# Staging rotary rows once per batch, and merging two norms into the projections behind them

## The reference, cut to what matters

```python
def _layernorm(x, axis=-1, eps=1e-05):
    ...
    return (x - m) / jnp.sqrt(v + eps)
...
c_kv = x @ W_kv_down
k_rope = _rotary_apply(c_kv @ W_k_rope, cos, sin)
k = (c_kv @ W_k_up).reshape(Bb, Tt, NH, HD)
v = (c_kv @ W_v_up).reshape(Bb, Tt, NH, HD)
q = (x @ W_q).reshape(Bb, Tt, NH, HD)
q_rope = _rotary_apply(x @ W_q_rope, cos, sin)
scores = jnp.einsum('bqhd,bkhd->bhqk', q, k)
scores = scores + jnp.einsum('bqr,bkr->bqk', q_rope, k_rope)[:, None]
...
w = jax.nn.softmax(scores, axis=-1)
attn = jnp.einsum('bhqk,bkhd->bqhd', w, v).reshape(Bb, Tt, D_MODEL)
```

## Time and profile before

| | us |
|---|---|
| median of three runs (3166.22 to 3172.92) | 3166.6 |
| the profiled execution, its time | 3168.85 |
| its span, first to last instruction | 3167.1 |
| PE busy in the span | 2359.3 (74%) |
| DVE busy | 1765.2 (56%) |
| ACT busy | 1243.2 (39%) |
| GpSimd (POOL) busy | 403.3 (13%) |

### The profile page before, as it was taken

The page is one execution under the profiler, slowest core; times in us unless marked ns, Lnnn a source line. Parts: engine busy times, 40 slices in busy tenths (PEclk is TensorE's granted clock), DMA queues, the critical chain, the costliest instruction groups (busy, mean ns, idle before and its releaser), DMA issues. The chain is left out here.

```text
span 3167.1 us, 47671 instructions
## 1 busy us (share of the span) xinstructions
PE 2359.3 (74%) x13512; PEld 1228.0 (39%) x13512; DVE 1765.2 (56%) x5580; ACT 1243.2 (39%) x1983; POOL 403.3 (13%) x452
## 2 busy tenths in 40 slices
PE   3649999999956328866999999999677292877382
PEld 1114344343335126532443434444254271554262
DVE  3746666666344896356665656666365324576223
ACT  2405555455525644553444444444222141343141
POOL 0000000000003000000000000000043463033554
PEclk9859999999968659967999999999888596888686
DMA  3272444443030000243121121121220142000144
GB/s 114 87 143 43 85 85 85 86 81 64 11 103 1 4 0 11 72 124 111 47 58 50 44 55 42 51 61 37 69 73 21 52 141 82 3 4 15 40 138 129
DMA packets 177888, 199.67 MB, mean 63 GB/s; under 512 B 36384, under 2 KB 117920, under 8 KB 177568
## 3 DMA queue, kind: packets, MB, share of 16 engines
q1 hardware_dynamic: 160000, 173.72, 22.0%
q0 software_dynamic: 9216, 19.02, 1.8%
q10 hardware_dynamic: 8448, 4.20, 0.4%
HBM read 127.09 MB, written 69.76 MB: 62 GB/s over the span
## 5 line engine op out<-in xcount | busy, mean ns | idle before, releaser
L910 ACT ACTIVATE at_probs<-at_score 128x1024 f32<-128x1024 f32 (+7 forms) x1024 | 654.7, 651 | 870.3 <-PE at_score L835 535.4
L935 DVE CUSTOM_DVE_ANT_0 at_masked<-at_mx,g_maskw 128x512 bf16<-128x512 f32 (+3 forms) x1024 | 483.3, 486 | 182.9 <-PE at_mx L801 178.2
L801 PE MATMUL at_mx<-at_K,at_Q 96*128 96x512 bf16 (+7 forms) x1536 | 464.9, 343 | 117.7 <-DVE at_mpart L935 39.6
L833 PE MATMUL at_score<-at_Q,at_K 96*128 96x512 bf16 (+7 forms) x1536 | 503.2, 332 | 27.7 <-issue 15.8
L835 PE MATMUL at_score<-at_Q,at_K 98*128 98x512 bf16 (+7 forms) x1536 | 506.3, 330 | 0.0
L931 DVE TENSOR_REDUCE at_mpart<-at_mx 128x1 f32<-128x512 f32 x512 | 353.8, 691 | 260.6 <-PE at_mx L801 242.1
L855 PE MATMUL at_outp<-at_probs,at_vop 128*32 128x512 f32 (+6 forms) x3072 | 445.9, 498 | 0.0
L801 PEld LDWEIGHTS at_mx<-at_K,at_Q 120*128 120x128 bf16 (+1 forms) x1536 | 148.2, 98 | 437.7 <-DVE at_mpart L935 198.2
L833 PEld LDWEIGHTS at_score<-at_Q,at_K 120*128 120x128 bf16 (+1 forms) x1536 | 149.5, 97 | 337.6 <-issue 180.9
L838 PE MATMUL at_score<-g_maskkq,g_identb 128*128 128x128 bf16 x1024 | 225.5, 221 | 0.0
L1025 POOL MEMSET n_spread<- 16x128 f32 (+1 forms) x2 | 0.7, 355 | 1537.9 <-POOLq L636 1537.9
(11 more groups left out here) (478 smaller groups left out, 3427.2 us busy)
## 6 DMA issues: line engine op xcount, KB each, us to landing
at_Q<-q SPq DMA_DIRECT2D x192, 128.0 KB, 2.8
at_Q<-qr SPq DMA_DIRECT2D x72, 256.0 KB, 6.7
at_K<-kr SPq DMA_DIRECT2D x72, 256.0 KB, 8.3
q<-p_pieces SPq DMA_DIRECT2D x40, 384.0 KB, 3.3
at_K<-k SPq DMA_DIRECT2D x168, 64.0 KB, 2.2
buf<-g_zeros SPq DMA_DIRECT2D x32, 325.0 KB, 5.3
o<-at_osb SPq DMA_DIRECT2D x64, 128.0 KB
n_oc<-o SPq DMA_DIRECT2D x8, 1024.0 KB, 5.0
```

The source lines that it names most:

```text
L801: pe.matmul(bank[:, 0:hi - lo], Q0[0:R, g % 4, j, qt * P:(qt + 1) * P], K0[0:R, g % 4, j % KG, lo:hi], start=True, stop=True).then_inc(s_m ...
L833: pe.matmul(bank, K0[0:R0, g % 4, j % KG, kb * P:(kb + 1) * P], Q0[0:R0, g % 4, j, lo:hi], start=True, stop=False)
L910: act.activation(probs[:, kb % 2, j, kb * P:T], src, ACT.Exp, scale=cf.scale).then_inc(s_exp, 1)
L935: dve.tensor_tensor_reduce(masked[:, u % 2, 0:w], mx[:, u % 2, 0:w], k.maskw[:, CH - w:CH], 1.0, NEG, ALU.add, ALU.max, mpart[:, part, j, ...
```

## The change

In the attention of the first layer, the 144 broadcast loads go. SP loads the rotary pieces of a batch once, unrepeated, into a tile `stage` of 96 partitions (12 loads of 64 KB). From there they are copied to the four heads of each slot by on-chip copies of 96 partitions x 4096 elements: for the first batch two by DVE (slot 0 of `Q0`, `K0`), four by ACT (both slots of `Q1`, `K1`), six by GpSimd; for the later batches all twelve by GpSimd, each pair behind the value products that free the slot. SP loads the next batch's `stage` at the end of a batch's first group. The starting memsets go from GpSimd to DVE in both attentions, and SP waits for the first of them alone; DVE's first `values` moves behind the first group's maxima.

In both projections the norm's block goes; `project` makes a `Norm` and weaves it in. The norm of chunk ch + 1 and the statistics of chunk ch + 2 are made while chunk ch is projected, and the bank of the latent product serves for the turned tiles too. The LO pieces go from DVE to GpSimd, which SP's stores and the next chunk's `rest` now wait for. The loops over chunks are written out.

```diff
+        if cf.SR:
+            stage = c.sb("stage", [96, 2, 2, T], BF16)
+            s_stage = c.sem("shared_staged")
...
-        nsh = 6 if cf.SR else 3
+        nsh = 3
...
+        def stage_loads(sp, b):
+            for p in range(2):
+                for n, (pieces, slots) in enumerate(((qs, Q_SLOTS), (ks, K_SLOTS))):
+                    for s in range(3):
+                        sp.dma_start(stage[32 * s:32 * s + 32, p, n, :],
+                                     pieces[slots[p][s], :, ds(first_token(b), T)]).then_inc(s_stage, 16)
+
         def shared_loads(sp, p, b, Qt, Kt, sem):
+            if cf.SR:
+                return
             for s in range(3):
                 r0 = 32 * s
                 def src(pieces, piece, n):
                     return pieces[piece, :, ds(first_token(b), T)].unsqueeze(1).broadcast_to([32, n, T])
-                if cf.SR:
-                    sp.dma_start(Qt[r0:r0 + 32, :, :], src(qs, Q_SLOTS[p][s], G)).then_inc(sem, 16)
-                sp.dma_start(Kt[r0:r0 + 32, :, :], src(ks if cf.SR else kp, K_SLOTS[p][s], KG)).then_inc(sem, 16)
+                sp.dma_start(Kt[r0:r0 + 32, :, :], src(kp, K_SLOTS[p][s], KG)).then_inc(sem, 16)
...
-            sp.wait_ge(s_set, 3)
+            if cf.SR:
+                stage_loads(sp, 0)
+            sp.wait_ge(s_set, 1)
...
+                if cf.SR and g == 0 and ahead(b, g, GN):
+                    for i in range(4):
+                        wait(s_s0[i], 2 * (b + 1))
+                    for i in range(2):
+                        wait(s_s1[i], 2 * (b + 1))
+                    stage_loads(sp, ahead(b, g, GN)[0])
...
-            pool.memset(K1[SHIFT_ROW:SHIFT_ROW + 2, :, :, :], 1.0).then_inc(s_set, 1)
-            pool.wait_ge(s_set, 1)
-            pool.memset(vop[:], 0.0).then_inc(s_set, 1)
-            pool.wait_ge(s_set, 2)
-            pool.memset(vop[:, :, :, :, d:d + 1], 1.0).then_inc(s_set, 1)
+
+            def spread(b, g, p):
+                Qt, Kt, sem = ((Q0[:, g % 4], K0[:, g % 4], s_s0[g % 4]) if p == 0 else
+                               (Q1[:, g % 2], K1[:, g % 2], s_s1[g % 2]))
+                pool.wait_ge(s_pv, (b * GN + g) * 8 + (8 if p == 0 else 24))
+                pool.sem_inc(s_ppassed, 1)
+                for n, t in enumerate((Qt, Kt)):
+                    pool.tensor_copy(t[0:96, :, :], stage[:, p, n, :].unsqueeze(1).broadcast_to([96, G, T])).then_inc(sem, 1)
+
+            def step(b):
+                pool.wait_ge(s_stage, 16 * 12 * (b + 1))
+                pool.sem_inc(s_ppassed, 1)
+                spread(b, 0, 0)
+                spread(b, 1, 0)
+                spread(b, 0, 1)
+                spread(b, 2, 0)
+                spread(b, 1, 1)
+                spread(b, 3, 0)
+
+            if cf.SR:
+                pool.wait_ge(s_stage, 16 * 12)
+                spread(0, 1, 0)
+                spread(0, 2, 0)
+                spread(0, 3, 0)
+                with pool.Fori(1, NB) as b:
+                    step(b)
...
-                    pe.wait_ge(s_s0[g % 4], 16 * nsh * (b + 1))
+                    pe.wait_ge(s_s0[g % 4], (2 if cf.SR else 16 * nsh) * (b + 1))
...
+            if cf.SR:
+                act.wait_ge(s_stage, 16 * 12)
+                for i in range(2):
+                    for n, t in enumerate((Q1, K1)):
+                        act.activation(t[0:96, i], stage[:, 1, n, :].unsqueeze(1).broadcast_to([96, G, T]),
+                                       ACT.Copy).then_inc(s_s1[i], 1)
...
+            dve.memset(K1[SHIFT_ROW:SHIFT_ROW + 2, :, :, :], 1.0).then_inc(s_set, 1)
+            dve.memset(vop[:], 0.0).then_inc(s_set, 1)
+            dve.wait_ge(s_set, 2)
+            dve.memset(vop[:, :, :, :, d:d + 1], 1.0).then_inc(s_set, 1)
+            if cf.SR:
+                dve.wait_ge(s_stage, 16 * 12)
+                for n, t in enumerate((Q0, K0)):
+                    dve.tensor_copy(t[0:96, 0], stage[:, 0, n, :].unsqueeze(1).broadcast_to([96, G, T])).then_inc(s_s0[0], 1)
+            reduce_units(0, 0, NARROW, 0)
+            wide_maxima(0, 0)
             dve.wait_ge(s_set, 3)
             values(0, 0)
-            reduce_units(0, 0, NARROW, 0)
-            wide_maxima(0, 0)
             reduce_units(0, 1, NARROW, 0)
...
+        norm = Norm(nc, c, k, xs, linear_view(hT), lambda ch: latp[:])
...
-            dve_steps += [("rest", n)] + [("lo", n - 1)] * (n > 0)
+            dve_steps += [("rest", n)]
         act_steps += [("mid", NI - 1)]
-        dve_steps += [("lo", NI - 1), ("values", 0)]
+        dve_steps += [("values", 0)]
...
+        turn_at = next((n for n in order if items[n].from_latent), None)
...
-                        sp.wait_ge(s_dve, DVN * (ch + 1) + dve_at["lo", n])
+                        sp.wait_ge(s_lo, NI * ch + n + 1)
...
+            norm.turn(pe, 0)
+            for i in range(NC // 2):
...
-                    pe.wait_ge(s_act, ACN * ch + act_at["lat", 0])
+                    pe.wait_ge(norm.s_ev, ch + 1)
...
+                        if n == turn_at:
                             pe.wait_ge(s_act, ACN * (ch + 1) + act_at["lat", 0])
+                            if ch + 1 < NC:
+                                norm.turn(pe, ch + 1)
...
+                    if turn_at is None:
+                        pe.wait_ge(s_act, ACN * (ch + 1) + act_at["lat", 0])
+                        if ch + 1 < NC:
+                            norm.turn(pe, ch + 1)
...
+            norm.root(act, 0)
+            norm.normalise_rest(act, 0)
+            norm.evacuate(act, 0)
+            norm.root(act, 1)
...
                             act.activation(lat[0:latent_rows, g, :], latp[0:latent_rows, :], ACT.Copy).then_inc(s_act, 1)
+                            if ch + 1 < NC:
+                                norm.normalise_rest(act, ch + 1)
+                            if ch + 2 < NC:
+                                norm.root(act, ch + 2)
...
                             act.activation(pcs[n][:, g, HI, :], source(n, it, g), ACT.Copy).then_inc(s_act, 1)
+                            if n == 0 and ch + 1 < NC:
+                                norm.evacuate(act, ch + 1)
...
+            norm.statistics(dve, 0)
+            norm.normalise(dve, 0)
+            norm.statistics(dve, 1)
...
+                    if ch + 1 < NC:
+                        norm.normalise(dve, ch + 1)
+                    if ch + 2 < NC:
+                        norm.statistics(dve, ch + 2)
...
+                            if ch > 0:
+                                dve.wait_ge(s_lo, NI * (ch - 1) + n + 1)
...
-                        elif what == "lo":
-                            dve.wait_ge(s_act, ACN * (ch + 1) + act_at["mid", n])
-                            dve.wait_ge(s_dve, base + dve_at["rest", n])
-                            ins = dve.tensor_tensor(pcs[n][:, g, LO, :], rest[0:it.rows, n, :], pcs[n][:, g, MID, :], ALU.subtract)
...
+        @block.gpsimd
+        def _(pool):
+            for ch in range(NC):
+                g = ch % 2
+                for n, it in enumerate(items):
+                    pool.wait_ge(s_act, ACN * (ch + 1) + act_at["mid", n])
+                    if ch >= 2:
+                        pool.wait_ge(s_st[g], 16 * NI * (ch // 2 + 1))
+                    pool.tensor_tensor(pcs[n][:, g, LO, :], rest[0:it.rows, n, :], pcs[n][:, g, MID, :],
+                                       ALU.subtract).then_inc(s_lo, 1)
...
-        hst, hT = normalised("l0")
-        with hst:
-            layer0_attention(nc, k, ins, scr, xs, hT)
+        layer0_attention(nc, k, ins, scr, xs)
...
-        hst, hT = normalised("l4")
-        with hst:
-            layer1_attention(nc, k, ins, scr, xs, hT)
+        layer1_attention(nc, k, ins, scr, xs)
```

More of the change, by code:

```diff
@@ L662, in attention @@
         s_mc, s_mrow, s_vop, s_oev = c.sem("max_chain"), c.sem("shift_turned"), c.sem("values_set"), c.sem("out_copied")
-        s_ms, s_passed = c.sem("shift_stored"), c.sem("sync_passed")
+        s_ms, s_passed, s_ppassed = c.sem("shift_stored"), c.sem("sync_passed"), c.sem("pool_passed")
         s_dpassed = c.sem("vector_passed")
@@ L875, in step @@
                 if g < 2:
-                    pe.wait_ge(s_s1[g % 2], 16 * nsh * (b + 1))
+                    pe.wait_ge(s_s1[g % 2], (2 if cf.SR else 16 * nsh) * (b + 1))
                 pe.wait_ge(s_mr[g % 2], 16 * (b * (GN // 2) + g // 2 + 1))
@@ L1115, in __init__, with project @@
         self.rows, self.w, self.from_latent, self.dst, self.w2 = rows, w, from_latent, dst, w2
-def project(nc, k, tag, hT, load, latent_w, latent_rows, items, make_values, vfree, split_latent=None, trig=None):
+def project(nc, k, tag, xs, load, latent_w, latent_rows, items, make_values, vfree, split_latent=None, trig=None):
     NI = len(items)
@@ L1128, in project @@
             cs = c.sb("cos_sin", [32, 2, T])
+        hT = c.sb("hT", [P, N])
         lat = c.sb("lat", [P, 2, CH])
@@ L1139, in project @@
         s_st = [c.sem(f"stored{i}") for i in range(2)]
```

(29 more changed lines are left out.)

4 lines of the change are left out of this document (removed).

## The result

The changed kernel takes 3180.05 us (median of 6 runs, 3178.44 to 3184.72), the kernel before 3166.41 in the same sessions (3165.48 to 3172.92): a ratio of 1.0038, interval 1.0028 to 1.0048. The forecast was 3163, 0.1% faster; measured is 0.4% slower. The profiled execution after has a span of 3177.6 us and a time of 3180.61, against 3167.1 and 3168.85: +10.5 in the span, +13.6 between the medians.

What follows compares the result with a forecast made beforehand. PE was taken to bound the rotary attention, DVE the projection before it. Terms -11.1 - 17.8 + 25 + 3 - 2 - 0.5 = -3.4 us gave 3165.5 profiled, 3163 on the median's basis; range 3120 to 3187.

Steps and rivals of the forecast that it cites:

- The mechanism that was given the most weight: Whole kernel: two wins at openings, paid back at group starts and in longer chunks; sum -3.4 us, chance 0.55.
- B: Group starts and projections: value operand and ring ops pass GpSimd's copies unheld, value operands 0.3 us; 3123 us, chance 0.27.
- C: Ten group starts: DVE held twice or more, 3.6 us more each, value operands over 4 us; 3199 us, chance 0.12.
- D: Projections: GpSimd becomes the bound at 2 us or more a piece, +20 us; 3183 us, chance 0.06.
- Opening of the rotary attention: Rotary attention's start: first product at 168, maxima chain unchanged at 44.2 us, scores at 212.2 instead of 229.97; -17.8 us.
- The head loads follow on SP and land meanwhile: Rotary attention's opening: head loads issued behind the stage loads land while DVE's memsets finish; no cost of their own given.
- The middle: Rotary attention's group starts: GpSimd's copy holds DVE's value operand, PE loses 2.5 us at ten starts; +25 us.
- First norm and projection: First stage: first product at about 39.5 (-18.6 us), chunks of 12.6 us and tail +7.5; net -11.1 us.
- Second norm, projection and the opening behind it: Second norm's block -22, norm's opening +5, longer chunks and tail +20, net +3; second attention's opening -2 us.
- GpSimd's pieces: Both projections: last pieces moved from DVE to GpSimd, taken at 1.0 us each, between 0.5 and 1.7.
- The copies of 96 x 4096 on GpSimd: Rotary attention: each GpSimd copy of 4096 elements priced at 3.6 us, from rows of 1024 and 512 elements.
- the likeliest case: Whole kernel: the forecast of 3163 us itself, chance 0.55, with its own range of 3149 to 3177.

## Why the prediction was wrong

The sum was -3.4 us on the profiled execution; the spans came out at +10.5. The mechanism that was given the most weight, two gains at openings paid back by held operations and longer chunks, is what happened. Rivals B, C and D did not: value operands of 2.64 to 2.74 us at group starts (B 0.3, C over 4), free masked maxima, pieces of 1.24 us (D 2 and more). What failed is the size of terms, the opening's above all.

- **Opening of the rotary attention: -17.8 forecast, -11.1 measured; half of the miss.** The step that failed is "From 162.6 + 2.2 to 162.6 + 8.0 the first product can start; I take 168". Three things behind it were wrong. Its basis, that DVE is free when the stage has landed: DVE's memsets start 1.6 us after SP's loads and end 11.0 us into the block, not 8.9. And the count of turns: not "some of the GpSimd copy" came between, but one ahead of each of DVE's copies, whole both times, so that two copies of 1.2 us of work took 9.1. Of the 6.5 us by which the first product is late (20.1 us in place of 168 - 154.4 = 13.6), 2.7 are the late start and 3.7 the turns. The forecast counted on GpSimd holding DVE at the group starts and let it do so only in part here, where both engines are given their copies at once. The third fault is hidden behind these two: "The head loads follow on SP and land meanwhile". They were held until 155.08, and with the turns taken away the first product still waited for them until 16.6 us after the first stage load. The chain of maxima behind it kept its length: 44.5 us, forecast 44.2.
- **The middle: +25 forecast, +23.8 measured, for partly other reasons.** Held value operands cost 2.4 us each, forecast 2.5. But seven starts, not ten: the first spread of each later batch waits for its stage loads and comes late, when nothing is there to hold. And at five of the seven the granted clock falls afterwards, another 1.4 us each, which the sum did not have. Two errors of some 7 us cancelled, so that the term is right by luck.
- **First norm and projection: -11.1 forecast, -7.9 measured.** The first product is 1.1 us later than forecast, 0.3 of it a slip in the sum (35.7 + 4.1 is 39.8, not 39.5). The chunk is 13.1, not 12.6: the hold was sized right (1.07; "+1.0 to 1.4"), the merged norm costs 14.30 - 11.04 = 3.26 (2.3 + 0.8 forecast), but the four pieces taken from DVE free 14.30 - 12.03 = 2.27, not "-2.8", because a piece takes 0.61 from start to start, not 0.69, and where one had stood DVE now waits 0.26 for ACT: 4 x 0.61 - 0.26 = 2.2.
- **Second norm, projection and the opening behind it: +1 forecast, +2.8 measured.** The hold was put at 1.2 us a chunk and is 2.3. Left out was the last rest: its source is the latent in SBUF, so that both its inputs are there, and it takes 1.48 us in place of 0.68. That the stage missed by 1.8 only is again luck: without the hold the chunk is 7.8 us, not the forecast's 8.2, and what lies outside the six chunks came out some 2 us better.
- **GpSimd's pieces** were taken at 1.0 us, between 0.5 and 1.7; they last 1.24 (128 partitions) and 1.15 (32). The Trainium skill, GPSIMD Engine Reference, 3.1, from which the prediction estimated 1.1 to 1.2, was the better source; the trace is near it.
- **The copies of 96 x 4096 on GpSimd** were worked out as 3.6 us and took 3.59 to 3.66 where no copy of DVE's fell between.

The remaining 1.5 + 1.2 us of the profile's difference lie in a stretch that the change does not touch and in the second attention behind its first load, where it moves little (the first value operand and the memsets of `vop`). Over all twelve profiles the first of these stretches, from the rotary attention's last output copy to the second feed-forward's end, took 460.6 to 464.2 us, the second 814.7 to 817.2, and the one behind the second attention's last output copy 896 to 902. No edit touches the first or the last, and I take all three for scatter between executions; but the three lowest times of the last belong to the three kernels with the reordered opening, and no run tells that from chance.

On the chances: "slower by over 0.2%" was given 0.28, and the whole range held the time; the likeliest case's own range, 3149 to 3177, missed it by 3 us. It reached for the opening's term from -14 to -21, too narrow for a term with two unknown prices in series.

The rule of the Trainium skill, SBUF - State Buffer, "SBUF: two separate sides", agrees with these traces in each of the cases below. The lock is for a whole instruction: 1.18 us of copy became 4.55 beside GpSimd's copies. A rest with one input in PSUM (0.69, at 1392.26) and a masked maximum (0.68) go free beside GpSimd; the rest with two inputs in SBUF does not.

## What to carry to other kernels

Work moved to GpSimd is not free just because GpSimd is idle: ask which SBUF-to-SBUF operations of DVE run at the moment it starts, and start it behind the one on the critical path; one such wait was worth 24 us here with the same copies done. At a stage's opening, several engines' preparations in series (memset, stage, copies, loads behind a wait) hide one another, so that removing one only shows the next: list them all with their start times before pricing any. And an in-order engine's step for a later chunk belongs behind the steps that the present chunk waits for.

## What was not expected of the hardware

- DVE and GpSimd alternate on copies from SBUF to SBUF: 1.18 to 1.22 us for 96 x 4096 bf16 on DVE alone, 4.55 and 4.61 with GpSimd copying; GpSimd 3.60 alone, 4.59 with one DVE copy between. The prediction took the DVE copy at 2.2. The Trainium skill, VectorE: DVE Perf Modes, "Side-by-side: where the cycles go for N=2048 bf16", gives about 693 ns for 2048 elements in the fastest mode: an estimate of at most 1.4 us for 4096 in proportion. The traces agree, with 1.18 to 1.22 for copies that read each row four times over from a stage.
- An idle of PE of 2.20 us was followed by a lower granted clock at five of seven starts and not at the other two. Each fall cost about 1.4 us (44.1 less 42.8). Over the seven profiles with held starts there is a pattern: the first held start of a batch, which follows a group that was not held, lost the clock in 2 of 21 cases, and the later ones, which follow a held group, in 28 of 28. Why is open. That the fall goes away with the idle is shown, as all these windows are at 1.00 when GpSimd's copies start behind the value operand.
- The same memset of 2 x 8192 bf16 takes 6.88 us on DVE and 6.92 on GpSimd: moving it from one to the other changes only what waits behind it.
